# Starting the experts of token chunk 0 directly behind the first attention

## What is computed

```python
# mixture of experts, on x already normalised once
normed = x * rsqrt(mean(x * x) + 1e-8) * norm_weight
shared = relu(normed @ sw1 + sb1) @ sw2 + sb2
probs = sigmoid(normed @ router_w.T)              # 8 routed experts
scores, idx = top_k(probs, 2)
w = scores / (sum(scores) + 1e-6)                 # comb: w at the two chosen experts, else 0
routed = sum over e of comb[e] * (relu(normed @ ew1[e] + eb1[e]) @ ew2[e] + eb2[e])
out = shared + routed
```

## Time and profile before

| | us |
|---|---|
| median of the 3 runs (lowest, highest) | 2072.73 (2071.41, 2072.86) |
| the profiled execution | 2074.85 |
| its span, first to last instruction | 2072.7 |
| PE busy, DVE, ACT, POOL | 1957.4, 1539.3, 1380.0, 982.9 |
| mean granted clock of PE | 0.973 |

### The profile page before, as it was taken

How to read it: one execution, slowest core, us unless ns; L and a number is a source line. 1 busy time by engine, 2 the same in 40 slices (tenths; PEclk the granted TensorE clock), 3 DMA queues, 4 the chain that set the end, 5 groups by cost and what they waited for, 6 DMA issues and landing times.

```text
span 2072.7 us, 37459 instructions
## 1 busy us (share of the span) xinstructions
PE 1957.4 (94%) x11698; PEld 1644.2 (79%) x11698; DVE 1539.3 (74%) x2851; ACT 1380.0 (67%) x2634; POOL 982.9 (47%) x1104
## 2 busy tenths in 40 slices
PE   4999999999999999679999799999999999999688
PEld 3878787878787877469999688888888888888566
DVE  5989898989898989822222777777777777777575
ACT  3878787878787878434443577777777777777355
POOL 2433333434343433410000577777777777778521
PEclk9999999999999999769999999999999999999798
DMA  4212121212121212100000000000000000100000
GB/s 110 47 43 47 43 46 42 46 42 46 42 46 42 46 42 44 47 14 1 0 0 0 8 4 9 4 8 3 8 3 10 0 10 0 63 1 1 1 1 21
DMA packets 36602, 51.04 MB, mean 25 GB/s; under 512 B 8361, under 2 KB 17586, under 8 KB 36146
## 3 DMA queue, kind: packets, MB, share of 16 engines
q1 hardware_dynamic: 36530, 50.15, 10.1%
HBM read 15.52 MB, written 1.05 MB: 8 GB/s over the span
## 4 chain that ended last, share of the span: by engine, by line
PE 82%; DVE 7%; issue 5%; POOL 4%; ACT 2%; DMA 1%; SPq 0%; DVEq 0%; POOLq 0%; ACTq 0%
PE ps_t L539 7%; PE ps_t L1008 6%; PE ps_o L549 6%; PE ps_s L1227 5%; PE ps_s L1228 5%; PE ps_s L1226 5%; PE ps_s L572 5%; PE ps_o L550 5%; PE ps_s L571 5%; PE ps_t L1280 3%; PE ps_o L1295 3%; PE ps_o L1296 3%; PE ps_o L1294 3%; POOL a_p L770 2%; PE ps_s L998 2%
## 5 line engine op out<-in xcount | busy, mean ns | idle before, releaser
L770 POOL TENSOR_SCALAR a_p<-a_p,a_rsum 128x1024 f32<-128x1024 f32 x256 | 289.4, 1130 | 515.2 <-DVE a_rsum L710 515.2
L1430 DVE TENSOR_REDUCE a_negmax<-ps_s 128x1 f32<-128x1024 f32 x256 | 312.3, 1220 | 67.5 <-PE ps_s L1228 65.0
L716 DVE TENSOR_REDUCE a_negmax<-ps_s 128x1 f32<-128x1024 f32 x256 | 313.5, 1225 | 50.6 <-PE ps_s L572 40.3
L1358 ACT ACTIVATE a_p<-ps_s,a_negmax 128x1024 f32<-128x1024 f32 x256 | 286.5, 1119 | 94.2 <-DVE a_negmax L1430 93.1
L647 ACT ACTIVATE a_pth<-ps_t 128x512 fp32r<-128x512 f32 x512 | 278.2, 599 | 101.3 <-PE ps_t L539 101.1
L695 DVE TENSOR_TENSOR a_ptl<-ps_t,a_pth 128x512 fp32r<-128x512 f32 x512 | 327.1, 680 | 11.2 <-ACT a_pth L647 7.1
L1531 POOL TENSOR_TENSOR a_p<-a_p 128x1024 f32<-128x1024 f32 x128 | 307.7, 2404 | 10.7
L677 ACT ACTIVATE a_p<-ps_s,a_negmax 128x1024 f32<-128x1024 f32 x256 | 288.4, 1127 | 1.3 <-DVE a_negmax L716 1.3
L539 PEld LDWEIGHTS ps_t<-ident_r,a_pr 128*128 128x128 f32 x2048 | 198.6, 141 | 65.4 <-DVE a_ptl L695 21.7
L539 PE MATMUL ps_t<-ident_r,a_pr 128*128 128x128 f32 x2048 | 222.9, 252 | 9.0 <-POOL a_p L770 8.4
L549 PE MATMUL ps_o<-a_pth,a_v 128*128 128x512 f32 x512 | 220.0, 430 | 1.6
(11 more groups left out here) (225 smaller groups left out, 4479.7 us busy)
## 6 DMA issues: line engine op xcount, KB each, us to landing
a_q<-a_kh SPq DMA_DIRECT2D x64, 128.0 KB, 2.2
a_q<-a_kl SPq DMA_DIRECT2D x64, 128.0 KB, 2.3
a_kh<-a_kh SPq DMA_DIRECT2D x64, 128.0 KB, 2.2
a_kl<-a_kl SPq DMA_DIRECT2D x64, 128.0 KB, 2.4
a_w_raw<-in_l_w SPq DMA_DIRECT2D x8, 384.0 KB, 3.0
f_raw<-in_ffn_w SPq DMA_DIRECT2D x2, 1408.0 KB, 7.5
f_w_raw<-in_ffn_w SPq DMA_DIRECT2D x9, 256.0 KB, 4.4
f_w<-in_ffn_w SPq DMA_DIRECT2D x1, 2304.0 KB, 9.0
```

Source lines behind the costliest of these rows:

```text
L716: dve.tensor_reduce(a0_negmax[:, s % 4:s % 4 + 1], ps_s[:, s % 2, :, :], AX.XY, ALU.max, negate=True)\
L770: pool.tensor_scalar(a0_p[s % 4][:, :], a0_p[s % 4][:, :], a0_rsum[:, s % 4:s % 4 + 1], 1.0, ALU.mult, ALU.mult).then_inc(S["a0_p_normed"], 1)
L1430: dve.tensor_reduce(a1_negmax[:, s % 2, m:m + 1], ps_s[:, m, :, :], AX.XY, ALU.max, negate=True)\
```

## The change

The experts of chunk 0 run straight behind the last attention head, and the rest of the prelude is spread over their matmuls.

- `a0_pe_out` makes the queries stationary and moves the weights, in 8 products of 128 x 128 instead of 2 of 128 x 512, so `Y` comes out with tokens down the partitions. `y0_turn` is gone, and the norms read `Y` in SBUF instead of PSUM.
- The norm of chunk 0 is made in the last three slots of the last head and in its tail; its turning stands between the last weighting and the last projection; chunk 1 follows behind it. Chunks 2 and 3 are normalised between expert additions of chunk 0 and turned after its seventh `up`.
- Experts run in the order shared, 0, ..., 7 (`f0_expert`). The shared expert's output needs no routing weight: ACT copies it into `Y`.
- Routing is made in two halves (chunks 0 and 1, then 2 and 3). The biases are made per chunk, at its third expert, and DVE adds them.
- First-layer weights are split one expert at a time. SP loads the small tensors early, and the second-layer weights in 9 DMAs that wait for the last weighting.
- PE's expert chunks are written out four times instead of looped. Buffers move so that nothing that runs together overlaps: the attention's value and weight buffers change places, and the second attention's small buffers now lie below its keys, at 94 KB.

The diff, cut (buffer lists, semaphore names, removed functions and the unchanged inner lines are left out):

```diff
         def a0_pe_out(pe, p, block):
 
             pe.wait_ge(S["a0_o_out"], p * 8 + (4 + block + 1))
-            pe.matmul(ps_m[:, :], a0_wo[0][:, :], a0_o[block][:, :], start=True, stop=False)
-            pe.matmul(ps_m[:, :], a0_wo[1][:, :], a0_o2[block % 2][:, :], start=False, stop=True)\
-                .then_inc(S["a0_out_in"], 1)
+            for i in range(TPC):
+                queries = slice(i * P, (i + 1) * P)
+                pe.matmul(ps_m[:, queries], a0_o[block][:, queries], a0_wo[0][:, :], start=True, stop=False)
+                ins = pe.matmul(ps_m[:, queries], a0_o2[block % 2][:, queries], a0_wo[1][:, :], start=False, stop=True)
+            ins.then_inc(S["a0_out_in"], 1)
...
-            pe.wait_ge(S["a0_exped"], g)
-            for c in range(2):
-                y0_turn(pe, c)
             for quarter in range(4):
                 a0_pe_pv(pe, n - 1, 1, 3, quarter)
                 if quarter == 1:
                     pe.wait_ge(S["a0_out_added"], 2 * H0 - 2)
                     a0_pe_out(pe, H0 // 2 - 1, 2)
+            f0_pe_turn(pe, 0)
             pe.wait_ge(S["a0_out_added"], 2 * H0 - 1)
             a0_pe_out(pe, H0 // 2 - 1, 3)
...
             pt_hi(g - 2, SLOTS - 2)
+            f0_act_w1_hi(act, 0)
             pt_hi(g - 1, SLOTS - 1)
             o_out(H0 // 2 - 1, 1, 2)
+            f0_act_turn(act, 0)
             o_out(H0 // 2 - 1, 1, 3)
...
+                    if last and s >= SLOTS - 3:
+                        if s == SLOTS - 3:
+                            dve.wait_ge(S["a0_out_added"], 2 * H0 - 3)
+                        y0_norm(dve, s - (SLOTS - 3), 0)
 
             a0_pairs(dve, body)
             g, n = H0 * SLOTS, 2 * H0
             rsum(g - 1, SLOTS - 1)
             pt_lo(g - 2, SLOTS - 2)
+            y0_norm(dve, 3, 0)
             pt_lo(g - 1, SLOTS - 1)
-            dve.wait_ge(S["y0_turned"], 2)
-            y0_norm(dve, 0, 0)
+            y0_norm(dve, 4, 0)
             add_out(n - 2, 2)
-            y0_norm(dve, 1, 0)
-            y0_norm(dve, 2, 0)
+            dve.wait_ge(S["a0_out_added"], n - 2)
+            y0_norm(dve, 0, 1)
+            f0_dve_turn(dve, 0)
             add_out(n - 1, 3)
...
+                    if last and s == SLOTS - 2:
+                        norm_rstd(pool, norm_a0(0, 0), 0)
                     if not (first and s < 1):
                         scale(g - 1, (s - 1) % SLOTS)
...
+            f0_load_small(sp)
...
+        def y0_norm(dve, stage, c):
+
+            n = norm_a0(c, stage >= 3)
+            x_tile = lambda k: tile(X, c * TPC + k)
+            y_tile = lambda k: tile(Y, c * TPC + k)
+            staged = lambda k: tile(xst[c % 2], k)
+            xc = X[:, c * TPC:(c + 1) * TPC, :]
+            if stage == 0:
+                norm_stats(dve, n, c, y_tile)
+            elif stage == 1:
+                dve.wait_ge(S["x_turned"], TURN_A0 + max(c - 1, 0))
+                norm_apply(dve, n, c, y_tile, staged).then_inc(S["dve_step"], 1)
+                dve_steps.next()
+            elif stage == 2:
+                dve.wait_ge(S["dve_step"], dve_steps.base + dve_steps.n)
+                dve.tensor_tensor(xc, xc, xst[c % 2][:, :, :], ALU.add).then_inc(S["dve_step"], 1)
+                dve_steps.next()
+            elif stage == 3:
+                dve.wait_ge(S["dve_step"], dve_steps.base + dve_steps.n)
+                norm_stats(dve, n, c, x_tile)
+            else:
+                norm_apply(dve, n, c, x_tile, staged).then_inc(S["xst_ready"], 1)
...
+        def f0_pe_turn(pe, c):
+
+            pe.wait_ge(S["xst_ready"], NC + c + 1)
+            if c == 3:
+                pe.wait_ge(S["x_hi"], TURN_A0 + 3)
+            turn_pe(pe, TURN_A0 + c, c, lambda i: xst[c % 2][:, i, :], f0_turn_bank(c))
...
+        def f0_act_turn(act, c):
+
+            if c == 0:
+                act.wait_ge(S["f0_small_loaded"], 16 * 4)
+            act.wait_ge(S["x_turned"], TURN_A0 + c + 1)
+            act.wait_ge(S["f0_logits"], from0(c - 1))
+            act.activation(f0_nT[c % 2][:, :], f0_turn_bank(c), ACT.Copy, scale=f0_nw[:, 0:1])\
+                .then_inc(S["f0_nT_ready"], 1)
+            turn_act(act, TURN_A0 + c, c, f0_nw[:, 0:1], f0_turn_bank(c))
...
+        def f0_expert(pos):
+
+            return (pos + NE - 1) % NE
+
+        def f0_act_w1_hi(act, pos):
+
+            e = f0_expert(pos)
+            act.wait_ge(S["f0_w1_loaded"][e], 16)
+            act.activation(f0_w1_hi[:, pos, :], f0_w1_raw[:, e, :], ACT.Copy).then_inc(S["f0_w1_hi_ready"], 1)
+
+        def f0_pool_w1_lo(pool, pos):
+            pool.wait_ge(S["f0_w1_hi_ready"], pos + 1)
+            pool.tensor_tensor(f0_w1_lo[:, pos, :], f0_w1_raw[:, f0_expert(pos), :], f0_w1_hi[:, pos, :], ALU.subtract)\
+                .then_inc(S["f0_w1_lo_ready"], 1)
...
+        def f0_act_probs(act, half):
+
+            act.wait_ge(S["f0_logits"], 2 * half + 2)
+            n = NT // 2
...
+        def f0_dve_route(dve, half):
...
+            n = NT // 2
+            t = slice(half * n, (half + 1) * n)
...
+            dve.wait_ge(S["f0_exped"], half + 1)
+            step(dve.tensor_scalar(f0_tmp[:, t, :], f0_prob[:, t, :], 1.0, None, ALU.add))
...
+        def f0_load_small(sp):
...
+        def f0_sp(sp):
+            sp.wait_ge(S["a0_pv"], 4 * H0)
+            for pos in range(NE):
+                first = pos < 2
+                sp.dma_start(f0_w2[:, pos, :, :], t["ffn0_w2"][:, f0_expert(pos), :, :])\
+                    .then_inc(S["f0_w2_first_loaded" if first else "f0_w2_loaded"], 16)
...
+                    if start and pos == 0:
+                        pe.wait_ge(S["f0_w2_first_loaded"], 16 * 2)
+                    if start and pos == 2:
+                        pe.wait_ge(S["f0_w2_loaded"], 16 * (NE - 2))
...
+                def weights_turn():
+
+                    if start:
+                        pe.wait_ge(S["f0_comb_ready"], 1)
+                    else:
+                        pe.wait_ge(S["f0_comb_ready"], 2)
+                        pe.wait_ge(S["f0_added"], from0(c * NE - (NE - 1)))
+                    for i in range(TPC):
+                        ins = pe.transpose(ps_o[0:NE, i * P:(i + 1) * P],
+                                           f0_comb[:, bass.ds(c * TPC + i, 1), :].rearrange("p a e -> p (a e)"),
+                                           ident[:, :])
+                    ins.then_inc(S["f0_combT_in"], 1)
...
+                    pe.wait_ge(S["f0_combT_ready"], c + 1)
+                    for i in range(TPC):
+                        ins = pe.matmul(ps_o[:, i * P:(i + 1) * P], f0_combT[:, i * P:(i + 1) * P], f0_b2[:, :],
+                                        start=True, stop=True)
+                    ins.then_inc(S["f0_bias_in"], 1)
+
+                for pos in range(NE):
+                    up(pos)
+                    if start and pos == 0:
+                        pe.wait_ge(S["a0_out_added"], 2 * H0)
+                        f0_pe_logits(pe, 0)
+                        f0_pe_turn(pe, 1)
+                    if start and pos == 1:
...
+                    if pos == 2:
+                        weights_turn()
+                    if pos:
+                        down(pos - 1)
+                    if pos == 2:
+                        bias()
+                    if start and pos == 6:
+                        pe.wait_ge(S["f0_added"], 1)
+                        f0_pe_turn(pe, 2)
+                        f0_pe_turn(pe, 3)
...
+            pe.wait_ge(S["x_lo"], TURN_A0 + 1)
+            chunk(0, True)
+            pe.wait_ge(S["x_lo"], TURN_F0)
+            for c in range(1, NC):
+                chunk(c, False)
...
+                    if start and pos == 0:
+                        f0_act_turn(act, 1)
+                    if start and pos < NE - 2:
+                        f0_act_w1_hi(act, pos + 2)
+                    if start and pos == 1:
+                        f0_act_probs(act, 0)
+                    if pos == 1:
+                        act.wait_ge(S["f0_down"], c * NE + 1)
+                        y = Y[:, bass.ds(c * TPC, TPC), :].rearrange("p t d -> p (t d)")
+                        act.activation(y, ps_t[:, 0, :], ACT.Copy).then_inc(S["f0_shared"], 1)
+                    if pos == 2:
+                        act.wait_ge(S["f0_combT_in"], c + 1)
+                        act.activation(f0_combT[:, :], ps_o[0:NE, :], ACT.Copy).then_inc(S["f0_combT_ready"], 1)
+                    if start and pos == 6:
+                        f0_act_turn(act, 2)
+                        f0_act_turn(act, 3)
+                if start:
+                    f0_act_probs(act, 1)
...
+            f0_act_w1_hi(act, 1)
+            chunk(0, True)
+            with act.Fori(1, NC) as c:
+                chunk(c, False)
...
+            for e in range(NR):
+                dve.memset(f0_rank[:, e:e + 1], float(NR - e))
+            dve.memset(f0_comb[:, :, NR:NE], 1.0).then_inc(S["dve_step"], 1)
```

(113 more changed lines are left out.)

218 lines of the change are left out of this document (59 added, 159 removed).

## The result

The changed kernel takes 2047.68 us (median; 2046.49 to 2050.9), the one before 2072.48 beside it (2071.41 to 2072.86): ratio 0.9885, interval 0.987 to 0.9901. The forecast was 2044.1, range 2036 to 2056, so the direction and the range held and the gain is 24.8 us, not 28.6. The profiled execution of after took 2046.49 (span 2044.5), the fastest of its four; that of before 2074.85 (2072.7). The first expert matmul comes 46.95 us earlier, and from it to the end of the experts it takes 19.3 us longer.

A forecast was written before the change was run, and what follows sets the result against it. A 59.84 us chain between attention and experts, hidden by no matmul, was what the change attacks. The sum 47.1 + 2.9 - 10.8 - 6.9 - 2.9 - 0.8 = 28.6 us off the median gave 2044.1, range 2036 to 2056.

The forecast's parts named there:

- The norm in the slots: Last three slots of the last head: chunk 0's norm on DVE delays the last weighting by 2.75 us, bounds 0 and 5.
- The projection's term: Attention's 32 output projections: the new shape costs 0.025 us each, 0.8 in all, bounds 0 and 12.
- step (2): Last weighting to last projection: 6.43 us before, plus 0.5 for turning chunk 0 on PE and 1.3 for ACT's copies.
- What is put between the matmuls: Expert stage on PE: logits 3.6, turnings 1.5, turned weights 2.1, biases 3.6, sum 10.8 us, bounds 8 and 21.
- Waits: PE's in-order queue in chunk 0: waits of 3.2, 0.8, 1.0, 0.4 and 1.5, sum 6.9 us, bounds 2 and 16.
- The clock: Behind the wait for turning chunk 1: one fall of the clock, charged 2.9 us, bounds 0 and 6.
- the limit of 80: Chunk 0 of the experts: the prediction is wrong if it takes over 80 us instead of 57.4 + 13.
- the span equals the median: Profiled execution of before: its span of 2072.7 equals the runs' median 2072.73, so the sum was applied to the median.
- DVE and POOL block each other: Rival, last head and chunk 0: DVE and POOL instructions lock each other out, costing 9.3 us, so 2053; chance 0.22.
- Nothing waits: Rival: the clock stays full and chunk 0's norm fits into idle time, 2.9 + 2.75 less, 2038; chance 0.08.
- Exposed loads: Rival, attention's projections: each stationary load costs 0.19 us, 43 us over 32 projections, so 2086; chance 0.04.
- It does not do what it says: Rival: an in-order wait keeps chunk 0 behind the other norms and routing, leaving some 3 us, 2070; chance 0.04.

The follow-up runs named there:

- fourth experiment: The changed kernel with chunk 0's norm stages moved from the last head's slots into its tail: 2049.79 us, ratio 0.9889 against before.
- experiments 9 and 11: ACT copies the last head's attention output before turning chunk 0: 9 on the eighth kernel, 2036.97 us; 11 on the changed kernel alone, 2045.51 us.
- Experiments 3, 5 and 7: Each on the changed kernel: 3 turns chunk 1 one `up` later, 2050.95 us; 5 puts POOL's roots one split later, 2045.07; 7 turns chunk 3 later, 2047.61.
- The eighth: The changed kernel with chunk 1 turned one `up` later, POOL's roots one split later and chunk 3 turned at the eighth expert: 2039.72 us, ratio 0.9844.
- tenth experiment: The changed kernel with fourteen unused products behind the first logits, filling PE's first wait: 2046.72 us, ratio 0.9885 against before.
- the first experiment: The changed kernel timed again with no edit: 2047.1 us, ratio 0.9877 against before.
- the second experiment: The kernel before with only the output projection's new shape, queries stationary: 2073.62 us, ratio 1.0007 against before.

## Why the prediction was right, and where its sizes were off

**What bounds the kernel.** Right. The 46.95 us by which the first expert matmul moved (47.1 in the sum, less 0.8 for the projections, so 46.3) are the gain; all else is what was paid for it.

**The start.** Three terms were off and cancel. The norm in the slots was put at 2.75 and came to 1.6 us net by the rows: +1.19 and +1.06 in its two slots, then 0.65 less from slot 15 to the last weighting (7.78 for 8.43). The fourth experiment agrees: with these stages out of the slots, slot 13 to the last weighting takes 14.22 us, against 15.66 in after and 14.06 in before. What failed here is the step that all work queued on DVE in the slots goes on the path. That the old turning of two chunks (L849), 0.94 us on PE ahead of the last weighting, is gone gives nothing back: in before it lay beside ACT's copy, which ended at 848.15, and in its place PE now waits 0.78 us for that copy (the row of 851.31), or 0.90 for DVE in the fourth experiment. The projection's term of 0.8 us was the second: it took 0.025 per projection from the rate of L1008, which runs in a row of 32; between scores and weighting it is 0.06, and the profiles have 1.5 to 2.2 in all. The third is an attention that began 0.58 us earlier (first row maximum 33.49 for 34.07), which was not forecast and whose cause is open. Of step (2), 0.5 and 1.3 us on PE and ACT, 1.7 showed (8.10 for 6.43); experiments 9 and 11 confirm the ACT part, by taking it away.

**What is put between the matmuls.** 10.8 forecast. By distances in the rows: logits 0.81 to 0.85 per chunk and turnings of 0.38 to 0.66, near what was said. Biases take 1.08 us for 8 products (886.00 to 887.08) and not 0.9, and `down` beside the turned weights 0.18 more; chunks 1 to 3, which hold nothing else, take 59.2 us each for 57.4 (from 935.5 to 1113.07). So weights and biases are 1.8 per chunk and not 1.4, and the whole is 11.8. The fault was to halve the biases' row from the low clock; for logits (0.81 for 1.78) and turned weights (0.44 for 0.90) halving was right.

**Waits.** 6.9 forecast, 7.76 measured, each at the place named: 3.90 for 3.2, 0.66 for 0.8, 1.37 for 1.0, 0.43 for 0.4, 1.40 for 1.5. The first was short by the path through DVE and POOL. Experiments 3, 5 and 7 between them take each away. The eighth has 2.12 left of them (0.75 at the turned weights, 1.37 at the sixth `up`), so it lacks 5.6 us; with the 1.5 of a fall of the clock that makes 7.1, and it is 7.4 to 8.0 faster than after.

**The clock.** The fall behind the first wait was forecast and came each time. It was charged at 2.9, as in before; the windows above lack 1.7 us of full clock behind the wait, and the tenth experiment prices it at 1.5. What had no place in the sum are the falls ahead of the first `up`, which come in some executions and not in others.

Chunk 0 took 74.3 us, under the limit of 80. The 70.4 named beside that limit has products and waits in it but not the fall of the clock; with its 2.9 the sum stands at 73.3. The last three slots grew by 1.6 us, under the limit of 5. From the first `up` to L1245 it is 251.89 us: 229.7 + 11.8 + 7.8 + 1.6 makes 250.9, and 1.0 is not assigned.

**The sum against the measured gain.** From profile to profile the gain is 28.4, and the sum was 28.6. But the medians say 24.8 (25.2 in the first experiment). The step that failed is "the span equals the median". In every execution, of before as of after, 2.0 to 2.2 us lie outside the span; so the profiled execution of before was itself 2.1 to 2.4 us over its median, and the profiled one of after was 1.2 under its own. The sum belonged to 2074.85, where it gives 2046.2 for the 2046.49 of after's profile. That this comes so close is in part luck, since the terms of the start cancel. The execution of before is the longest of 36 (the others take 2070.16 to 2074.15), and its mean clock of 0.973 is the lowest, shared by two that took 2072.82 and 2073.10. Why its clock was low isn't known.

**Rivals.** *DVE and POOL block each other*: the long rows are there, their price is not. The timeline of after, both engines:

```profile
851.57 1.29 POOL L918 TENSOR_TENSOR f_w_lo<-f_w_raw,f_w_hi 128x512 fp32r<-128x512 f32 x1
...
851.63 2.08 DVE L306 TENSOR_SCALAR xst<-X,mv,rstd 128x128 f32<-128x128 f32 x4 [0.47 <-POOL rstd L332]
...
867.76 1.11 DVE L306 TENSOR_SCALAR xst<-X,mv,rstd 128x128 f32<-128x128 f32 x4 [1.94 <-POOL rstd L332]
```

Four applies beside a split took 2.08 us, 1.11 alone. This agrees with what the Trainium skill says in "SBUF — State Buffer", section "SBUF: two separate sides", that such instructions of DVE and GpSimd shut each other out. But chunk 1's apply, which the rival had at 3.9 us more, met no split, and the one that met it (851.63) ended 3.1 us before its turning. One meeting did fall on the path, at 0.3 us: in slot 14 the apply took 1.43 us beside POOL's scaling, where the same four from `Y` take 1.12 alone (862.55). What did reach PE from POOL is its queue: 1.8 us at the fifth and seventh `up`, which the own sum had at 1.4. *Nothing waits* is refuted by the brackets; its time, 2038, lies by the eighth kernel (2039.7), which still waits for 2.1 us. *Exposed loads* is refuted by the second experiment, at most 2.2 us for 43. *It does not do what it says* by the first `up` at 861.

## What to carry to other kernels

When the bound engine's queue is in order, look for its first wait, but move it only after asking who is queued behind the late work: the same edit cost 2 us by the rows (3.9 by the medians) with POOL's queue as it was and gained 4 with it changed. A sum worked out from one profiled execution is to be set against that execution's own time, and what the medians will show is less certain than the sum by the spread between executions. At the hand-over from one stage to the next, putting the copy that PE needs first ahead of two others on ACT (0.6 to 0.7 us each) was worth 1.6 us.

## What the hardware showed beside this

The same kernel ran with one stretch at 1.2 GHz in one execution and three in another, each behind a wait of 1.5 to 4 us on PE: behind 3.4 to 3.9 us in six profiles of six, behind 1.5 and 2.0 us in seven of nineteen places. Filling the long wait with products kept the clock up there (tenth experiment), at no cost and for no measured gain. And one kind of small product was not worth half of its row at the low clock: eight bias products of nine partitions took 1.08 us against 1.80 at half clock.
